# Small-head attention handed to the output projection without a trip through DRAM, and its values stored in whole rows

## The reference, cut to what matters

```
h = layernorm(x) * (1 + ca) + sa
q, k, v = h @ Wq.T + bq, h @ Wk.T + bk, h @ Wv.T + bv     # each [4, 512, 32 heads, 16]
scores = einsum('bshd,bsgd->bshg', q, k) / 4              # heads against heads, per token
scores = where(scores > 0.001, scores, -inf)
out = einsum('bshg,bsgd->bshd', softmax(scores), v)       # [4, 512, 512]
x = x + ga * (out @ Wo.T + bo)
h = layernorm(x) * (1 + cb) + sb
x = x + gb * lora_ffn(h)       # a router picks one of 8 experts of rank 16
```

## Time and profile before

| | us |
|---|---|
| median of 3 runs | 2467.64 |
| the profiled execution | 2484.07 |
| its span | 2482.4 |
| QKV stage, first pass | 1021.91 to about 1120 |
| attention stage, first pass | 1120.51 to about 1198 |
| finish stage, first pass | 1198.09 to about 1273 |
| attention stage, second pass, first load | 2329.91 |

### The profile page before, as it was taken

How to read it: one execution, slowest core, us unless ns; L and a number is a source line. 1 busy time by engine, 2 the same in 40 slices (tenths; PEclk the granted TensorE clock), 3 DMA queues, 4 the chain that set the end, 5 groups by cost and what they waited for, 6 DMA issues and landing times. The chain is left out here.

```text
span 2482.4 us, 34071 instructions
## 1 busy us (share of the span) xinstructions
PE 2040.4 (82%) x11760; PEld 1654.6 (67%) x11760; DVE 1531.3 (62%) x3721; ACT 1009.0 (41%) x2344; POOL 1082.7 (44%) x830
## 2 busy tenths in 40 slices
PE   7489999999999953676647999999999999419557
PEld 1378888888888842555326888888888887317444
DVE  1666666666666678426645666666666666781456
ACT  1255555555555530113024555555555555120311
POOL 0455554544545534304226455555545554341223
PEclk9699999999999986785768999999999999659559
DMA  5300001001000001596230100001001000019851
GB/s 234 111 18 26 18 27 43 18 26 43 18 26 32 29 22 63 15 80 157 73 120 27 35 24 26 18 26 43 18 27 43 18 26 18 30 55 31 150 135 43
DMA packets 157928, 123.82 MB, mean 50 GB/s; under 512 B 75173, under 2 KB 119205, under 8 KB 156725
## 3 DMA queue, kind: packets, MB, share of 16 engines
q1 hardware_dynamic: 146836, 104.96, 21.2%
q10 hardware_dynamic: 10912, 16.60, 2.0%
HBM read 100.27 MB, written 21.27 MB: 49 GB/s over the span
## 5 line engine op out<-in xcount | busy, mean ns | idle before, releaser
L970 POOL TENSOR_TENSOR gqa_rot<-gqa_rot,consts 128x512 f32<-128x512 f32 x160 | 209.2, 1307 | 640.1 <-ACT gqa_rot L791 640.0
L807 ACT ACTIVATE gqa_prob<-gqa_prob,gqa_nmax 128x128 f32<-128x128 f32 (+3 forms) x512 | 281.9, 552 | 198.5 <-DVE gqa_nmax L892 198.5
L892 DVE CUSTOM_DVE_ANT_0 gqa_prob<-gqa_pS,consts 128x128 f32<-128x128 f32 (+3 forms) x512 | 220.2, 486 | 73.8 <-PE gqa_pS L691 73.0
L900 DVE TENSOR_TENSOR gqa_ptl<-gqa_pT,gqa_pth 128x384 fp32r<-128x384 f32 (+1 forms) x384 | 218.3, 596 | 31.7 <-ACT gqa_pth L817 27.2
L817 ACT CAST gqa_pth<-gqa_pT 128x384 fp32r<-128x384 f32 (+1 forms) x384 | 182.6, 511 | 94.4 <-PE gqa_pT L706 94.4
L973 POOL TENSOR_TENSOR gqa_full<-gqa_full,gqa_rot 128x512 f32<-128x512 f32 x160 | 206.7, 1292 | 12.6
L745 PE MATMUL gqa_pW<-woh,gqa_oh 128*128 128x512 f32 x504 | 202.7, 402 | 9.0 <-DVE first_y L917 9.0
L435 PE MATMUL ln_pT<-consts,ln_xn 128*128 128x128 f32 x192 | 45.3, 424 | 197.5 <-DVE ln_xn L414 197.5
L664 PE MATMUL gqa_pj<-first_hh,wqh 128*128 128x512 f32 x496 | 205.3, 414 | 0.0
L745 PE MATMUL gqa_pW<-woh,gqa_ol 128*128 128x512 f32 x504 | 197.3, 391 | 0.0
L745 PE MATMUL gqa_pW<-wol,gqa_oh 128*128 128x512 f32 x504 | 196.5, 390 | 0.0
(11 more groups left out here) (205 smaller groups left out, 5136.1 us busy)
## 6 DMA issues: line engine op xcount, KB each, us to landing
raw_q<-in_wq SPq DMA_DIRECT2D x16, 1024.0 KB, 5.3
raw_o<-in_wo SPq DMA_DIRECT2D x16, 1024.0 KB, 5.2
mod_wm<-in_wmod SPq DMA_DIRECT2D x8, 1536.0 KB, 19.8
raw_kv<-in_wkv SPq DMA_DIRECT2D x16, 512.0 KB, 6.6
vp<-qkv_rest SPq DMA_DIRECT2D x64, 68.0 KB, 10.9
heads_bd<-vp SPq DMA_DIRECT2D x64, 68.0 KB, 3.1
x<-in_x SPq DMA_DIRECT2D x4, 1024.0 KB, 6.3
kp<-qkv_rest SPq DMA_DIRECT2D x16, 256.0 KB, 3.1
```

What stands on the lines that cost most here:

```text
L807: ins = nc.scalar.activation(p, p, ACT.Exp, scale=-1.0, bias=nmax[r][:, i:i + 1], accum_out=den[r][:, i:i + 1])
L892: nc.vector.tensor_tensor_reduce(prob[r][:, P_OFF[i]:P_OFF[i] + w], pS[s][:, c:c + w], held.mask[:, T - w:T], -1.0, LARGEST, ALU.add, ALU.min,
L900: nc.vector.tensor_tensor(ptl[:, c:c + w], pT[k % 2][:, 0:w], pth[:, c:c + w].bitcast(F32), ALU.subtract).then_inc(pt_lo, 1)
L970: nc.gpsimd.tensor_tensor(rot[r % 2][:], rot[r % 2][:], held.sinT, ALU.mult).then_inc(sined, 1)
```

## The change

QKV_ORDER becomes keys, queries, values. The values are stored by one DMA per tile in whole rows of 512 floats, four tokens interleaved, so that the blocks of the units are contiguous in token order; the ones are no longer stored. The attention stage reads the values with four DMAs per unit, 32 partitions by 32 tokens by 16 floats, and sets the ones itself, in four small memsets per buffer. The first `kd` buffer lies where y of layer 0 lies, and POOL clears it in the QKV stage. Each batch has its own `o`, kept in SBUF into the finish stage; the stores and loads of `attn` are gone. Wo is held as [d, 512] for each head on its partition, four times, once for each block of 32 partitions: four DMAs of 1 MB, behind the new loads of bias and gates (class OutBias), at the same place, u == 3. POOL multiplies and adds the bias in the attention stage, one operation behind each subtraction from chunk 6 on. In the finish stage the projection is 16 products of 32 rows for each 128 tokens, the loop over d outside and the four token blocks inside, into four banks; the former bank pW is one of the four and its users stand in the order of use.

```diff
-QKV_ORDER = (2, 1, 0)
+QKV_ORDER = (1, 0, 2)
...
-        self.w = sb("out_w", [P, KT, D])
+        self.w = sb("out_w", [P, D1, D])
...
-        sp.dma_start(self.w[:], self.a["w1o"].rearrange("(k p) n -> p k n", p=P)).then_inc(self.came, 16)
+        for j in range(4):
+            sp.dma_start(self.w[32 * j:32 * j + 32], self.a["w1o"].rearrange("(d h) n -> h d n", h=H1)).then_inc(self.came, 16)
...
+class OutBias:
...
+    def load(self, sp):
+        sp.dma_start(self.bo[:], self.a["b1o"].rearrange("(o d) -> o d", o=1).to_broadcast([P, D])).then_inc(self.came, 16)
+        for which, gate in ((2, self.ga), (3, self.gb)):
+            for b in range(HB):
+                sp.dma_start(gate[:, b, :], self.a["gates"][which, bass.ds(self.half * HB + b, 1), :].to_broadcast([P, D])
+                             ).then_inc(self.came, 16)
...
                     if w == 2:
-                        for r in range(4):
-                            sp.dma_start(a["vp"][b, r, :, :, m].rearrange("g l x -> l g x"),
-                                         values(n)[r * LO:(r + 1) * LO]).then_inc(stored[n % NB], 16)
+                        dst = a["vp"][b].rearrange("(t r) x -> r t x", r=KT)[m]
+                        sp.dma_start(dst, src[:]).then_inc(stored[n % NB], 16)
...
+                nc.gpsimd.memset(kd0[:], 0.0).then_inc(k_zeroed, 1)
...
-        kd = [st.sb(f"kd{i}", [P, 4, 4 * LU, H1]) for i in range(NU)]
+        kd = [kd0] + [st.sb(f"kd{i}", [P, 4, 4 * LU, H1]) for i in range(1, NU)]
...
             for r in range(4):
-                src = a["vp"][b, r, :, l0:l0 + LU].rearrange("g l j x -> g (l j) x")
-                eng.dma_start(bd[u % NU][32 * r:32 * r + 32, r], src).then_inc(v_in[u], 16)
+                t0 = (LO * r + l0) * KT
+                src = a["vp"][b, t0:t0 + KT * LU, :].rearrange("t (g x) -> g t x", g=H1)
+                eng.dma_start(bd[u % NU][32 * r:32 * r + 32, r, :, 0:D1], src).then_inc(v_in[u], 16)
...
                     if u == NU:
-                        for weights in ahead:
+                        for weights in (ob,) + ahead:
                             weights.load(sp)
-                for b in range(HB):
-                    store(b)
-                sp.wait_ge(o_out, 64 * HB)
...
-                    if b and l0 == 0:
-                        dve.wait_ge(o_out, 64 * b)
-                    nc.vector.tensor_tensor(o[:, :, :, l0:l0 + LC].rearrange("p x j l -> p l j x"), pO[c % NO][:, :, :, 0:D1],
+                    nc.vector.tensor_tensor(o[b][:, :, :, l0:l0 + LC].rearrange("p x j l -> p l j x"), pO[c % NO][:, :, :, 0:D1],
...
-                nc.vector.memset(kd[0][:], 0.0).then_inc(k_zeroed[0], 1)
                 nc.vector.memset(bd[0][:], 0.0).then_inc(v_zeroed[0], 1)
+                dve.wait_ge(v_zeroed[0], 1)
+                for r in range(4):
+                    nc.vector.memset(bd[0][32 * r:32 * r + 32, r, :, D1:], 1.0).then_inc(ones[0], 1)
...
+                    if c >= CHUNKS - HB - NT:
+                        n = c - (CHUNKS - HB - NT)
+                        if n == 0:
+                            ob.landed(pool)
+                        if n < HB:
+                            nc.gpsimd.tensor_tensor(ob.bg[:, n], ob.bo[:], ob.ga[:, n], ALU.mult).then_inc(ob.gated, 1)
+                        else:
+                            j = n - HB
+                            pool.wait_ge(ob.gated, j // TT + 1)
+                            nc.gpsimd.tensor_tensor(held.x[:, j, :], held.x[:, j, :], ob.bg[:, j // TT], ALU.add).then_inc(ob.biased, 1)
...
-        ps = [st.ps(f"ps{i}", [P, D]) for i in range(3)]
+        ps = [st.ps(f"ps{i}", [P, D]) for i in range(4)]
...
                     for j in range(b * TT, (b + 1) * TT):
                         wait_bank(pe, "o", j)
-                        for k in range(KT):
-                            pe.wait_ge(a_in[b][k], 16)
-                            mm = pe.matmul(bank("o", j)[:], at[:, k, j * P:(j + 1) * P], out.w[:, k, :],
-                                           start=(k == 0), stop=(k == KT - 1))
-                        mm.then_inc(o_full, 1)
+                    for d in range(D1):
+                        for j in range(TT):
+                            q = slice(32 * j, 32 * j + 32)
+                            mm = pe.matmul(bank("o", b * TT + j)[:], o[b][q, d].rearrange("p r l -> p (r l)"), out.w[q, d],
+                                           start=(d == 0), stop=(d == D1 - 1))
+                            if d == D1 - 1:
+                                mm.then_inc(o_full, 1)
```

More of the change, by code:

```diff
@@ L1068, in stage_qkv @@
         flat = [st.sb(f"flat{i}", [P, T]) for i in range(NB)]
-        rest = [st.sb(f"rest{i}", [P, H1 * VW]) for i in range(NB)]
+        rest = [st.sb(f"rest{i}", [P, T]) for i in range(NB)]
         ps = [st.ps(f"ps{i}", [P, T]) for i in range(8)]
-        w_lo, b_scaled, ones, full, left, turned = (st.sem(n) for n in ("w_lo", "b_scaled", "ones", "full", "left", "turned"))
+        w_lo, b_scaled, full, left, turned = (st.sem(n) for n in ("w_lo", "b_scaled", "full", "left", "turned"))
         stored = [st.sem(f"stored{i}") for i in range(NB)]
+        k_zeroed = st.sem("k_zeroed")
         items = [(w, b, m) for w in QKV_ORDER for b in range(HB) for m in range(KT)]
         N = len(items)
-        NV = HB * KT
-        total, stored_by = [0] * NB, []
-        for n, (w, b, m) in enumerate(items):
-            total[n % NB] += 64 if w == 2 else 16
-            stored_by.append(total[n % NB])
-        def values(n):
-            return rest[n % NB][:].rearrange("p (g x) -> p g x", g=H1)
+        FIRST_V = 2 * HB * KT
         with nc.Block() as block:
@@ L1192, in stage_head_attention @@
         k_zeroed, v_zeroed = [st.sem(f"k_zeroed{i}") for i in range(NU)], [st.sem(f"v_zeroed{i}") for i in range(NU)]
+        ones = [st.sem(f"ones{i}") for i in range(NU)]
         s_full, copied, top_done, shifted, exp_done, masked, turned = (st.sem(n) for n in (
@@ L1195, in stage_head_attention @@
         o_full, recip, o_left, o_out = st.sem("o_full"), st.sem("recip"), st.sem("o_left"), st.sem("o_out")
-        for weights in ahead:
+        for weights in ahead + (ob,):
             weights.sems(st)
@@ L1345, in _ @@
                     nc.gpsimd.memset(bd[i][:], 0.0).then_inc(v_zeroed[i], 1)
+                    pool.wait_ge(v_zeroed[i], 1)
+                    for r in range(4):
+                        nc.gpsimd.memset(bd[i][32 * r:32 * r + 32, r, :, D1:], 1.0).then_inc(ones[i], 1)
+                        pool.wait_ge(ones[i], r + 1)
                 for c in range(CHUNKS):
@@ L1507, in weights_left @@
                     act.wait_ge(w_turned, b + 1)
[L1508 removed]
+                    nc.scalar.copy(wtT[:, b], bank("w", b)[:]).then_inc(w_left, 1)
                 features(0)
@@ L1635, in build @@
                     stage_norm(nc, held, a, 1, 0, half, residual=1, ahead=qkv)
-                    stage_qkv(nc, held, a, qkv)
+                    stage_qkv(nc, held, a, qkv, kd0)
             with ExitStack() as octx:
+                osb = lambda n, s, dt=F32: octx.enter_context(nc.sbuf_tensor(n, s, dt))
+                o = [osb(f"o{b}", [P, D1, 4, LO]) for b in range(HB)]
                 out = OutWeights(octx, nc, a)
                 lora = LoraWeights(octx, nc, a)
-                stage_head_attention(nc, held, a, (out, lora))
-                stage_finish(nc, held, a, out, lora, half)
+                ob = OutBias(octx, nc, a, half)
+                stage_head_attention(nc, held, a, (out, lora), ob, kd0, o)
+                stage_finish(nc, held, a, out, lora, ob, o, half)
 def kernel(**inputs):
```

111 lines of the change are left out of this document (42 added, 69 removed).

## The result

The changed kernel takes 2488.99 us (median of 4 runs, 2484.14 to 2491.83) beside 2468.98 for the kernel before (median of 4 runs, 2465.37 to 2470.64): a ratio of 1.0081, 95% interval 1.0064 to 1.0098. It is 0.8% slower, where the prediction said 2456.8 and most likely faster. One execution of the kernel before, in a later comparison, took 2947.88 us at a granted clock of 0.668, against 0.89 to 0.90 in all others; it is compared with nothing here. The profiled execution is one of those four runs, 2489.12 around a span of 2487.4.

What follows compares the result with a forecast made beforehand. TensorE was busy 82% of the span, but waits for stores and loads in each pass's last stages were taken to count. Terms -24.1+9.4+9.3 = -5.4 us a pass, -10.8 for two, took the median 2467.64 to 2456.8; range 2436 to 2520.

Steps and rivals of the forecast that it cites:

- the QKV term: QKV stage: with whole-row value stores the wait for vp stores goes and the stage shortens, -24.1 us a pass.
- the Wo block: Attention stage: Wo, bias, gates and LoRA queued before unit 4's keys delay chunk 8 from t=32.3 to 53.1, +20.8 us.
- The value gathers: Attention stage: reading values in 64-byte pieces takes 4.0 us a unit; later units need 6.6 us of DMA, +2.2 us.
- Bias on POOL: Attention stage: POOL's added 1.44 us bias operation just fits in a chunk from chunk 6 on; +1 us for slips.
- No trip through DRAM: Attention output: the 4.83 us wait for the store of o goes, -4.6 us; output product 0.9 us after o.
- The projection: Finish stage: 15.8 us a batch, 7 us idle between batches, up-projection starting at 56.6 instead of 47.3, +9.3 us a pass.
- The sum: One pass: -24.1 (QKV), +9.4 (to first output product), +9.3 (projection) = -5.4 us; two passes -10.8.
- Wide Wo: Rival, attention stage: 32-partition loads run at 385 GB/s, block 10 us shorter a pass, total 2437 us; chance 10%.
- slow gathers: Rival, attention stage: value gathers as slow as the stores, 8.2 us each, pass +25 us, total 2518; chance 20%.
- products at the low clock: Rival, output projection: clock stays low, a batch costs 27.5 us, +23.4 a pass, total 2504; chance 12%.
- unshared ones: Rival, output projection: 32-row products do not share the array, a batch costs 55 us, total 2612; chance 3%.
- Sharing less than fourfold: Rival, output projection: 1.3 slots for each one planned, +8.2 us a pass, total 2473; chance 13%.

Runs made afterwards that it cites:

- the control: The kernel before, run again unchanged: median 2468.98 us over 10 runs; QKV stage 88.2 us to the attention stage's first load.
- the second queue: The joined version with the value gathers of rows 64 to 127 on ACT's queue: 2415.18 us, and 2412.60 when run again.
- the joined version: Changed kernel with Wo loaded in the QKV stage, separate PSUM banks per projection batch, and LoRA last in the attention stage's queue: 2415.45 us, 2416.57 again.
- eight banks: Changed kernel with batch 0 of the output projection summing into the four PSUM banks that the transposes use later: 2464.74 us.
- The version that joins what the runs taught: The joined version with the value gathers of rows 64 to 127 on ACT's queue, run again: 2412.60 us.

## Why the prediction was wrong, step by step

The step that failed is the QKV term, -24.1 us a pass: the runs show -14.3 and -13.6. With -14.3 in its place the prediction's own sum is -14.3+9.4+9.3 = +4.4 a pass, slower, about 2476 us. The second miss is the size of the Wo block: +20.8 us for chunk 8 was planned, and against the control it is +29.1 (62.6-33.5) in the first pass and +24.7 in the second.

*The base and the QKV term.* Here the sign was lost. The new stage came out at 73.9 us (74.5 planned) with no vp wait. But -24.1 was taken from one execution in which the old stage took 98.6, and in two others it took 88.2 and 87.5. That the execution stood 16 us above the median was written down, and the difference was then carried over as a constant ("its intervals are short enough that I apply the difference to the median"). It wasn't one: it lay in the term that the change removes. Of -48 us over both passes, 20 were never there. The prediction's "second runs within 1 us of it" was misread too: in its own profile chunk 8 stands at 34.2 in the second pass against 32.3, and the first output product at 82.8 against 80.4.

*The value gathers (4.0 us a unit).* Right in size: later units follow every 6.5 us (6.6 planned; 7.1 in the second pass), and chunk 6 starts within 1 us of the control. That they are what holds those units is shown by the second queue, which brings them to 5.9 and 6.2.

*The block of Wo.* The rate was right (195 to 197 GB/s, 201 planned), and the mechanism is confirmed by removing the block; its size came out too small. Chunk 8 came at t=62.6 (59.1 in the second pass) instead of 53.1. Some 4 us of it lie ahead of Wo, whose pieces, as an estimate from the rates of the windows, began around 1128.3 (t=30.6, planned 26.4) and ended around 1149.5 (t=51.8). Bias and gates, which come just before, were priced at 385 GB/s, and from 1124 to 1130 the windows of 1 or 2 us show 202 to 274. The other 5 us are behind Wo: 1.4 us for LoRA, 2.6 for keys and 1.8 to land became 10.8. The likely error was to price queued loads one after another at their lone rates, where the 64-byte gathers of unit 3 and the key loads share the engines (169, then 62 GB/s); that is read from the windows and the issues, and no run isolates it.

*Bias on POOL.* +1 was planned, some 0.6 measured in the joined version.

*No trip through DRAM.* Right: the first output product comes 1.5 us after the last output operation starts (11.3 in the control), and the 4.83 us wait is gone.

*The projection.* Right within 1 us throughout: 15.6 us a batch (15.8 planned), 7.0 of idleness (7), up-projection after 56.4 (56.6, though the steps that the prediction lists add up to 56.4). Against the control's 46.7 that is +9.7 in the one pass and 57.1-48.0 = +9.1 in the other. The bank wait that was foreseen is nearly its whole price: with eight banks the up-projection comes after 48.1 us.

*The sum.* Against the control the first pass has -14.3 (QKV), +17.4 (to the first output product) and +8.5 (from there), together +11.6; the second -13.6+14.5+8.5 = +9.4. That is 21.0 us of the 23.1 between the two spans; the rest is spread over stages that the change doesn't touch. The prediction had -5.4 a pass; +10 of the miss come from the QKV term and +5 to +8 from the block.

*The rivals.* Wide Wo is refuted (197 GB/s; with the source named four times it is slower still), and so are slow gathers, products at the low clock (1.00 after the start) and unshared ones. Sharing less than fourfold doesn't show: 96 products in 10 us are one per 0.104 us, and four per 0.42 us is one slot. The Trainium skill ("TensorE: Matmul & The Clock Gate", Part 3) gives 3.07; this stream of 128 products shows four. None of the rivals named the mechanism that decided, a term of the kernel before that was read from an unusual execution. That 2488.99 lies inside the stated range is luck: the range's upper end came from slow gathers, which didn't occur.

## What to carry to other kernels

When the profiled execution is longer than its median, find the stage that is long before using any of its waits as a gain, above all if the change removes that wait; a second profile of the unchanged kernel shows it. When a change adds loads, add up the transfers of the stage beside its compute: here 47 us of products could no longer hide 74 and more of DMA, spreading inside the stage gained 10 us, and moving the loads to a neighbouring stage whose queue had room gained 47. The version that joins what the runs taught takes 2412.6 us, 2.2% below the kernel before, so the change's parts paid once its loads lay in the right place. If all sums of a batch end together, let the next batch have its own banks: that was worth some 9 us a pass here.

## What was not expected of the hardware

Loads into 32 partitions ran at 195 to 201 GB/s on one queue, at 213 to 214 on two queues within the same half of the partitions, and at 353 to 375 when the two in flight went to different halves (the 353 by inference from the issue times). Loads that name their source four times through a leading broadcast ran at 100 GB/s and a DMA share of 0.26. Three issues of SP behind 4 MB of queued loads took 5 us each, where one behind less took 0.56, and the keys behind them were issued only after that. And the QKV stage with its 68-byte stores, whose engines worked for 84 to 85 us in two executions (first pass), took 95 in another of the same kernel, with nothing changed.
